# The statistics of three of four images move beside the first chunk's projections, and the last chunk prepares no successor

## The reference

```python
xn = layernorm(gn(x)) * ln_w + ln_b              # over channels
xb, z = split(xn @ w_in.T)                       # 384 -> 2 x 768
xc = silu(causal_conv4(xb) + conv_b)
dt, B, C = split(xc @ w_x.T)                     # 24, 16, 16
dt = softplus(dt @ w_dt.T + dt_b)
h = exp(dt * A) * h + (dt * xc) * B              # 16 states for each of 768 channels, along 4096 steps
y = (sum_n h * C + xc * D) * silu(z)
x = x + y @ w_out.T
x = x + attention(gn(x))                         # 8 heads of 48, windows of 64 positions, and a projection
```

## Time and profile before

| | us |
|---|---|
| median of 3 runs (6865.48 to 6866.52) | 6866.09 |
| the profiled execution, its own time | 6863.25 |
| its span | 6861.5 |
| two statistics blocks at the start | 0 to 74 |
| preparation of chunk 0 | 74 to 187.7 |
| 32 chunks of scan, 167.3 on average | 187.7 to 5542 |
| output of chunk 31, statistics | 5542 to 5574 |
| attention | 5574 to 6861.5 |

### The profile page before, as it was taken

One profiled execution on the slowest core, in us unless ns is written; L12 is line 12 of the kernel. 1 busy time (PEld: TensorE's weight loads), 2 busy tenths in 40 slices (PEclk: granted clock), 3 DMA queues, 4 the chain that ended last, 5 costly groups with the idle time before them and its releaser, 6 DMA issues. The chain is left out here.

```text
span 6861.5 us, 99209 instructions
## 1 busy us (share of the span) xinstructions
PE 5990.6 (87%) x32906; PEld 3756.6 (55%) x32906; DVE 6138.1 (89%) x7731; ACT 4716.2 (69%) x8759; POOL 5351.3 (78%) x4333
## 2 busy tenths in 40 slices
PE   4888888888888888888888888888888879999998
PEld 2455555555555555555555555555555547777776
DVE  4899999999999999999999999999999956666665
ACT  1777777777777777777777777777777743333332
POOL 0999999999999999999999999999999930101010
PEclk9999999999999999999999999999999989999999
DMA  4322222222222222222222222222222232222222
GB/s 186 114 112 111 112 109 112 102 101 101 100 102 101 101 101 103 104 101 102 100 101 102 100 101 104 104 101 102 101 101 101 108 125 71 78 79 77 81 73 68
DMA packets 177702, 694.99 MB, mean 101 GB/s; under 512 B 28332, under 2 KB 28556, under 8 KB 143140
## 3 DMA queue, kind: packets, MB, share of 16 engines
q1 hardware_dynamic: 177188, 688.65, 27.0%
HBM read 512.57 MB, written 157.09 MB: 98 GB/s over the span
## 5 line engine op out<-in xcount | busy, mean ns | idle before, releaser
L774 POOL TENSOR_TENSOR dbx<-u,bb 128x512 f32<-128x512 f32 x3072 | 3829.4, 1280 | 29.9 <-DVE p_da L673 14.8
L673 DVE TENSOR_TENSOR_SCAN p_da<-p_da,state_v,dbx 128x512 f32<-128x512 f32 x2112 | 2620.8, 1273 | 54.6 <-ACT p_da L548 54.6
L548 ACT ACTIVATE p_da<-dt,neg_a 128x512 f32<-128x512 f32 x3076 | 2076.1, 687 | 83.6 <-DVE h L680 8.2
L898 PEld LDWEIGHTS p_yt<-ident,hc_v 128*128 128x128 f32 x8448 | 1108.8, 151 | 1137.1 <-issue 843.0
L898 PE MATMUL p_yt<-ident,hc_v 128*128 128x128 f32 x8448 | 1381.5, 293 | 162.9 <-DVE hc_v L689 162.4
L689 DVE TENSOR_TENSOR hc_v<-cc,p_da 128x512 f32<-128x512 f32 x2112 | 1391.4, 666 | 0.0
L783 POOL TENSOR_TENSOR hc_g<-h,cc 128x512 f32<-128x512 f32 x960 | 1227.6, 1279 | 108.4 <-DVE h L680 108.3
L680 DVE TENSOR_TENSOR_SCAN h<-p_da,state_g,dbx 128x512 f32<-128x512 f32 x960 | 1218.1, 1269 | 103.8 <-ACT p_da L548 103.5
L839 PE MATMUL p_g<-xs,win 128*128 128x512 f32 x2376 | 1208.6, 603 | 74.7 <-ACT zt L500 36.3
L554 ACT ACTIVATE state_v<-p_da 128x1 f32<-128x1 f32 x2112 | 351.0, 166 | 914.2 <-DVE hc_v L689 901.8
L1321 POOL TENSOR_TENSOR x_low<-axn,x_upper 128x512 fp32r<-128x512 f32 x96 | 127.3, 1355 | 1045.9 <-DVE x_upper L1273 1045.9
(11 more groups left out here) (153 smaller groups left out, 7397.5 us busy)
## 6 DMA issues: line engine op xcount, KB each, us to landing
bb<-bc_spill SPq DMA_DIRECT2D x132, 1024.0 KB, 10.4
cc<-bc_spill SPq DMA_DIRECT2D x132, 1024.0 KB, 10.2
xc_spill<-xc SPq DMA_DIRECT2D x99, 512.0 KB, 2.6
z_spill<-zt SPq DMA_DIRECT2D x99, 512.0 KB, 3.9
xj<-xc_spill SPq DMA_DIRECT2D x193, 256.0 KB, 4.1
zj<-z_spill SPq DMA_DIRECT2D x192, 256.0 KB, 2.7
xs<-in_x SPq DMA_DIRECT2D x34, 768.0 KB, 5.7
xc<-in_x SPq DMA_DIRECT2D x33, 768.0 KB, 11.9
```

Of the source, the lines that this page charges most:

```text
L548: nc.scalar.activation(p_da[n % RD][:], dt[:, d % 2, :], ACT.Exp, scale=neg_a[:, d, n:n + 1])\
L673: nc.vector.tensor_tensor_scan(psum, psum, dbx[:, n % RB, :], state_v[:, d, k:k + 1], ALU.mult, ALU.add).then_inc(s_scan, 1)
L774: nc.gpsimd.tensor_tensor(dbx[:, n % RB, :], u[:, d % 2, :], bb[:, n, :], ALU.mult)\
L898: last = nc.tensor.matmul(p_yt[d % 2][:, b * P:(b + 1) * P], product[:, b * P:(b + 1) * P], ident[:], start=False, stop=n == NS - 1, is_tr ...
```

## The change

`input_statistics` becomes `constants` and loads nothing; the block of `group_affine` "in" is gone. In `scan_layer` SP first loads `win`, `lnb`, `lnw`, then the 8 tiles of image 0 into eight slots that lie in `bb` (5) and `cc` (3), `x[0]`, the other eight weights, and then the 24 tiles of the other images, of which tile c waits until VectorE is done with tile c - 8. VectorE takes image 0's statistics and its affine (part 0) ahead of `scale(0)`, and the 72 statistics instructions of the other images after `normalise(0)`, while TensorE and ScalarE do chunk 0's projections. Their affine (part 1) is put into chunk 0's scan, at g = 0, 2, 5 on VectorE, 1 on TensorE, 4 on ScalarE. SP fills `bb` and `cc` for chunk 0 when all statistics are done. The load of x[1] moves from ahead of `xj` to behind the first quarter of B, and `scale(1)` behind the first four decays. The pass i = 31 leaves out all that it did for a 33rd chunk, and `load_residual(NCH)` waits for x1 of chunk 31 alone.

```diff
--- before.py
+++ after.py
+AFFINE_STEPS, AFFINE_AT = 1 + 1 + 3 + 1 + 2, (0, 1, 2, 4, 5)
...
         gsc = ctx.enter_context(nc.sbuf_tensor("gsc", [P, NCH], F32))
         gbi = ctx.enter_context(nc.sbuf_tensor("gbi", [P, NCH], F32))
-        input_statistics(nc, x, ident, quarter, mean_w, eps_col, stats)
-        group_affine(nc, "in", stats, quarter, eps_col, gsc, gbi)
+        constants(nc, ident, quarter, mean_w, eps_col, stats)
-                   xc_d, z_d, bc_d, x1_d, ident, mean_w, eps_col, stats, gsc, gbi)
+                   xc_d, z_d, bc_d, x1_d, ident, quarter, mean_w, eps_col, stats, gsc, gbi)
...
-def input_statistics(nc, x, ident, quarter, mean_w, eps_col, stats):
-    RX = 4
+def constants(nc, ident, quarter, mean_w, eps_col, stats):
...
+        x_slots = [bb[:, NJ * r:NJ * r + NJ, :] for r in range(5)] + [cc[:, NJ * r:NJ * r + NJ, :] for r in range(3)]
+        RX = len(x_slots)
...
+        af_m, af_v = p_g[1][:, 0:NBATCH], p_g[1][:, NBATCH:2 * NBATCH]
...
-        N_LOADS = 11
+        N_LOADS = 8
...
         def _(sp):
+            def load_stat_x(c):
+                if c >= RX:
+                    sp.wait_ge(s_sd, (c - RX + 1) * NJ)
+                sp.dma_start(x_slots[c % RX], x[c]).then_inc(s_sx[c % RX], 16)
+            for dst, src in ((win, w_in), (lnb, ln_b), (lnw, ln_w)):
+                sp.dma_start(dst[:], src).then_inc(s_wi, 16)
+            for c in range(CPB):
+                load_stat_x(c)
             sp.dma_start(xs[:], x[0]).then_inc(s_xl, 16)
-            for dst, src in ((win, w_in), (wx, w_x), (wdt, w_dt), (wout, w_out), (cw, conv_w), (cb, conv_b),
-                             (dtb, dt_b), (dsk, d_skip), (neg_a, a_log), (lnw, ln_w), (lnb, ln_b)):
+            for dst, src in ((wx, w_x), (wdt, w_dt), (wout, w_out), (cw, conv_w), (cb, conv_b),
+                             (dtb, dt_b), (dsk, d_skip), (neg_a, a_log)):
                 sp.dma_start(dst[:], src).then_inc(s_w, 16)
+            for c in range(CPB, NCH):
+                load_stat_x(c)
...
-                sp.wait_ge(s_xm, i + 1)
-                for k in range(2):
-                    sp.wait_ge(s_xcs[k], i * 16 + 16)
+                if i < NCH:
+                    sp.wait_ge(s_xm, i + 1)
+                    for k in range(2):
+                        sp.wait_ge(s_xcs[k], i * 16 + 16)
+                else:
+                    sp.wait_ge(s_os, i * 16)
                 sp.dma_start(back, x[(i + (NCH - 1)) % NCH]).then_inc(s_rl, 16)
...
             for k in range(3):
                 store_silu(0, k)
-            load_x(1, 1)
             sp.wait_ge(s_xcs[0], 16)
             sp.dma_start(xj[:], xc_d[0, :, 0, :]).then_inc(s_xjl, 16)
             store_bc(0)
             sp.wait_ge(s_bcs, 16)
+            sp.wait_ge(s_sd, NCH * NJ)
             for k in range(4):
                 load_b(0, k)
+                if k == 0:
+                    load_x(1, 1)
...
-                    if 2 <= d < 5:
+                    if 2 <= d < 5 and q < NCH:
                         store_silu(q, d - 2)
-                    if d == 5:
+                    if d == 5 and q == NCH:
+                        load_zj(i, d)
+                    elif d == 5:
                         load_xj(q, 0)
-                        load_x(q + 1, (q + 1) % NCH)
+                        if q + 1 < NCH:
+                            load_x(q + 1, q + 1)
                         store_bc(q)
                         sp.wait_ge(s_bcs, q * 16 + 16)
...
+            def affine(part):
+                act.wait_ge(s_afm, 2 * part + 2)
+                images = slice(0, 1) if part == 0 else slice(1, NBATCH)
+                nc.scalar.activation(af_rs[:, images], af_v[:, images], ACT.Ln, bias=eps_col[:, 0:1]).then_inc(s_afa, 1)
+                act.wait_ge(s_afa, 2 * part + 1)
+                nc.scalar.activation(af_rs[:, images], af_rs[:, images], ACT.Exp, scale=-0.5).then_inc(s_afa, 1)
+            affine(0)
+            act.wait_ge(s_afd, AFFINE_STEPS)
             for j in range(NJ):
                 scale(0, j)
             act.wait_ge(s_w, 16 * N_LOADS)
@@ -571,12 +600,12 @@
                 if k % 6 == 5:
                     silu(0, k // 6)
             copy_xd(0)
-            for j in range(NJ):
-                scale(1, j)
             softplus(0, 0)
             skip(0, 0)
             for n in range(RD):
                 decay(0, 0, n)
+            for j in range(NJ):
+                scale(1, j)
...
-                        else:
+                        elif after[0] < NCH:
                             decay(*after, n + RD - NS)
+                        if i == 0 and d * NS + n == AFFINE_AT[3]:
+                            affine(1)
                         if n == COPY_Y_AT:
                             copy_y(i, d)
-                        if n == SOFTPLUS_AT:
+                        if n == SOFTPLUS_AT and after[0] < NCH:
                             softplus(*after)
-                        if n == SKIP_AT:
+                        if n == SKIP_AT and after[0] < NCH:
                             skip(*after)
                         g = d * NS + n
-                        if g in SCALE_AT:
+                        if g in SCALE_AT and q + 1 < NCH:
                             scale(q + 1, SCALE_AT.index(g))
+                        if q == NCH:
+                            continue
...
+            def input_stats(c):
+                dve.wait_ge(s_sx[c % RX], c // RX * 16 + 16)
+                for j in range(NJ):
+                    at = (c + 1) * (NJ * 6) + j * 6
+                    nc.vector.bn_stats(stats[:, at:at + 6], x_slots[c % RX][:, j, :]).then_inc(s_sd, 1)
+            def affine_means(part):
+                first, last = (0, 1) if part == 0 else (1, NBATCH)
+                dve.wait_ge(s_sd, last * CPB * NJ)
+                for b in range(first, last):
+                    at, per = (b * CPB + 1) * (NJ * 6), CPB * NJ * 6
+                    nc.vector.bn_aggr(af_mv[:, b, :], stats[:, at:at + per]).then_inc(s_afd, 1)
+                done = part * AFFINE_STEPS + last - first
+                dve.wait_ge(s_afd, done)
+                nc.vector.tensor_copy(af_mean[:, first:last], af_mv[:, first:last, 0]).then_inc(s_afd, 1)
+            def affine_variance(part):
+                at = slice(0, 1) if part == 0 else slice(1, NBATCH)
+                done = part * AFFINE_STEPS + (2 if part == 0 else NBATCH)
+                dve.wait_ge(s_afm, 2 * part + 1)
+                nc.vector.tensor_tensor(af_dev[:, at], af_mv[:, at, 0], af_m[:, at], ALU.subtract).then_inc(s_afd, 1)
+                dve.wait_ge(s_afd, done + 1)
+                nc.vector.tensor_tensor(af_sq[:, at], af_dev[:, at], af_dev[:, at], ALU.mult).then_inc(s_afd, 1)
+                dve.wait_ge(s_afd, done + 2)
+                nc.vector.tensor_tensor(af_sq[:, at], af_sq[:, at], af_mv[:, at, 1], ALU.add).then_inc(s_afd, 1)
+            def affine_result(part):
+                first, last = (0, 1) if part == 0 else (1, NBATCH)
+                at = slice(first, last)
+                done = part * AFFINE_STEPS + (5 if part == 0 else NBATCH + 3)
+                dve.wait_ge(s_afa, 2 * part + 2)
+                nc.vector.scalar_tensor_tensor(out=af_bi[:, at], in0=af_m[:, at], scalar=-1.0, in1=af_rs[:, at],
+                                               op0=ALU.mult, op1=ALU.mult).then_inc(s_afd, 1)
+                dve.wait_ge(s_afd, done + 1)
+                for dst, src in ((gsc, af_rs), (gbi, af_bi)):
+                    wide = src[:, at].rearrange("p (b o) -> p b o", o=1).to_broadcast([P, last - first, CPB])
+                    nc.vector.tensor_copy(dst[:, first * CPB:last * CPB].rearrange("p (b c) -> p b c", c=CPB), wide)\
+                        .then_inc(s_afd, 1)
+            for c in range(CPB):
+                input_stats(c)
+            affine_means(0)
+            affine_variance(0)
+            affine_result(0)
+            dve.wait_ge(s_wi, 16 * 3)
+            dve.wait_ge(s_prepm, 1)
+            for j in range(NJ):
+                nc.vector.tensor_scalar(win[:, j, :], win[:, j, :], lnw[:, j:j + 1], None, ALU.mult)\
+                    .then_inc(s_prep, 1)
             for j in range(NJ):
                 centre(0, j)
             dve.wait_ge(s_w, 16 * N_LOADS)
@@ -706,13 +789,12 @@
                 for k in range(TAPS):
                     nc.vector.tensor_scalar(cdiag[:, t, k, :], ident[:], cw[:, t, k:k + 1], None, ALU.mult)\
                         .then_inc(s_prep, 1)
-            dve.wait_ge(s_prepm, 1)
-            for j in range(NJ):
-                nc.vector.tensor_scalar(win[:, j, :], win[:, j, :], lnw[:, j:j + 1], None, ALU.mult)\
-                    .then_inc(s_prep, 1)
             dve.wait_ge(s_prep, N_PREP)
             for j in range(NJ):
                 normalise(0, j)
+            for c in range(CPB, NCH):
+                input_stats(c)
...
                             keep_state(i, d, BY_POOL.index(n) // RH)
```

(46 more changed lines are left out.)

36 lines of the change are left out of this document (16 added, 20 removed).

## The result

The changed kernel takes 6805.52 us (median of 5, 6802.13 to 6807.46), the one before 6866.09 in the same session: 60.6 us less, a ratio of 0.991 (95% interval 0.9896 to 0.9924). Forecast: 6805, with 60.9 us of gain.

What follows compares the result with a forecast made beforehand. VectorE was taken to bound the scan loop, and a serial one-engine-at-a-time chain the first 187.7 us. 61.2 + 3.0 - 7.0 + 3.0 + 0.7 = 60.9 us off the median 6866.1 gives 6805.2; 8-in-10 range 6797 to 6814.

Steps and rivals of the forecast that it cites:

- Statistics of image 0: Opening: eighth tile loaded at 26.9 us, its statistics done at 28.8, affine with one bn_aggr done at 32.6.
- cover of the bias matmuls: Opening: 72 bias matmuls end near 27, before TensorE's first affine matmul at 29.7; 2.7 us to spare.
- To the first in_step: From the affine's end to the first in_step: 51.9 us against 113.1, gain 61.2; clock -3 to +3.
- The other 24 tiles: 45 us of VectorE statistics after the first in_step, ending at 97, due near 117: hidden, cost nothing.
- So 0, up to 2: SP's first store queued behind statistics loads, issued 7 us late, landing 4 to 7 us after issue: cost 0 to 2 us.
- B, C and x[1]: Ahead of the first scan: B's first quarter no longer behind x[1]'s 768 KB; gain 3.0 us, bounds 0 and 4.
- The later quarters come 1 us sooner, which the next item hides: B and C loads for chunk 0: later quarters come 1 us sooner, not 3, hidden by the affine's part 1.
- Affine, part 1: Chunk 0's pass: 3.3 us added VectorE work plus 3.7 us wait for mean at centre; loss 7.0, bounds 3.3 and 9.
- The last pass: No 33rd chunk prepared: VectorE's work falls below GpSimd's; gain 3.0 us, between 0 and 6.2.
- The clock rival: Last pass and tail: TensorE's clock drops, VectorE waits 1 us a gate, tail loses 2.0; 6811 us, chance 0.15.
- The tail: After the loop: load_residual(NCH) no longer queued behind broadcasts, so residual starts earlier; gain 0.7 us.
- Passes 1 to 30: Scan loop between chunk 0's pass and the last: no change, 0 us.

Runs made afterwards that it cites:

- run 5: Changed kernel with win, lnb and lnw loaded behind image 0's eight tiles and x[0]; 6819.5 us, first scan 13.3 us later.
- run 8: Changed kernel with VectorE's six operations of 0.6 us put back into the last pass, results unused; last pass 163.0 us against 159.9, time 6804.40.
- run 4: Changed kernel with the first store of xc and zt put ahead of the last three statistics loads on SP; 6807.95 us, first scan 2.1 us earlier.
- run 2: Changed kernel with mean(1) ahead of the affine part 1's second matmul on TensorE; pass 0 172.9 us instead of 176.1, time 6802.66.
- run 9: Changed kernel once more, without any edit; 6806.22 us.
- run 1: Kernel before the change with only the 33rd chunk left out, opening not edited; 6863.45 us against 6865.21, ratio 0.9996.
- run 3: Changed kernel with the affine's part 1 taken out of chunk 0's scan and put ahead of it; 6797.32 us (median of 4), pass 0 170.7 us.
- run 6: Changed kernel with affine part 1 ahead of the scan, plus x[1]'s load moved behind the second store of xc and zt; 6795.68 us, pass 0 166.6.
- run 10: Changed kernel with every statistics instruction of the 24 tiles of images 1 to 3 done twice; 6830.93 us, first scan 27.7 us later.

## Why the prediction was right, step by step

- **Statistics of image 0.** Right: aggregate at 28.89 (28.8), affine done at 32.7 (32.6), cover of the bias matmuls 2.2 (2.7), its price shown by run 5.
- **To the first in_step.** 1.6 us better than forecast, all of it TensorE's clock: `mean` took 4.71 us instead of 5.49, `variance` 4.5 instead of 5.5. The text had set 3 us aside for this. In the other executions with this opening the first in_step came at 50.3 to 51.1.
- **The other 24 tiles.** Right that they hide: VectorE was done at 92.9. "So 0, up to 2" for SP's queue: taken at 0, it was 1.7 where TensorE kept the clock that it had before (run 8 against run 4), within the bound. The landing was mis-sized, 9.6 us where 4 to 7 stood; the copy was 3.7 us late in run 8, and TensorE's second bank took about half of that.
- **B, C and x[1].** In the first profile 1.9 of the "gain 3.0" came: from the copy of `xd` on, 61.0 us of lead became 62.9. That profile was an unlucky one. From the copy of `xd` to the first scan it took 11.0 us, and runs 2, 5, 8 and 9, with the same code there, 10.1 to 10.3; the kernel before took 12.9 and run 1, alike there, 13.1. So the gain is 2.6 to 3.0, as forecast. The +0.1 of the table is the 1.9 less the 1.8 that the projections lost (run 4). The store of B and C took 3.4 to 3.5 us, not 3.0, and was issued 0.5 us later in the first profile than in those four. Why it took longer than 3.0 is not shown; the last stores of `xc` and `zt` were issued just ahead of it. "The later quarters come 1 us sooner, which the next item hides" was right that they were hidden, and missed that x[1] among them was itself a delay of 4.1 us for whoever takes the cover away (runs 3 and 6).
- **Affine, part 1.** Right in mechanism, short by 2.5 us: 9.5 where 7.0 stood, beyond the bound of 9. The centre's wait was as reckoned, 3.9 for 3.7 (run 2 takes back 3.3). Missing were the wait for ScalarE's result, 1.4 us, and 0.7 us of work, 4.0 where 3.3 stood, as the sum at L758 took 1.1 us. Work and both waits add up to 9.3 of the 9.5. Why that sum is slow in the loop no run shows; ahead of the loop it took 0.16 us on the same three columns (run 3).
- **The last pass.** Right in sign, 5.0 for 3.0, within the bounds. VectorE's own work counts nearly in full (run 8). The reason given for stopping at 3.0, that VectorE's work falls below GpSimd's, did not come about: 160.8 us against 159.4 in the window of 162.3. The clock rival was right about the clock, 0.70, and wrong about its price: VectorE waited 0.3 us for TensorE in the whole pass.
- **The tail.** The DMA's wait is gone, but in the first profile the twelve passes took 8.43 us, for the most part at the lower clock. Net nothing there, and 1.4 us more were lost behind it. Both depend on the execution. Of the eleven traces with this tail, seven have the twelve passes at 8.4 to 8.5 us, and four, runs 2, 3, 8 and 10, at 6.8 to 6.9. In those four `residual` starts 13.3 to 13.4 us behind the last scan (15.0 in the seven, 14.9 before), and from there to the end it takes 1309.7 to 1310.1 us (1311.5 to 1311.7 in the seven, 1310.1 before). Between 60 and 100 us behind the last scan the granted clock is 0.95 in the four and 0.87 in the seven. So the gain of 0.7 was real and more, up to 1.6, when the clock was up, and this stretch alone moves the time by over 3 us. What decides between the two is not shown. `residual` in run 2:

```profile
5491.19 0.69 DVE L691 TENSOR_TENSOR xc<-xc,p_g 128x512 f32<-128x512 f32 x1 [6.92 <-PE p_g L963]
```

- **Passes 1 to 30.** Unchanged but for 0.8 us: after a disturbed pass the next ones are shorter (166.6, 166.9, 167.2, then 167.25). Executions of kernels alike in these passes differ by up to 5.4, so the 0.8 says nothing of the change.

## What to carry to other kernels

Work moved "beside" a serial stretch is cheap only if it stays out of the bound engine's stream behind it: here ten instructions of 0.14 to 1.1 us at the head of the loop made its first pass 9.5 us longer, and nothing was lost when they were put into the 31.8 us that VectorE idled just ahead of it and x[1] was out of the way too (run 6). Price a multi-engine chain by the waits it puts in front of what stands behind each of its links, on the transfer queue too: twice the statistics made not their own end late but a store that stood behind their loads. Once a wait is removed, look for the next one it had covered. And before a difference of 1 to 2 us in one trace is explained, look for other executions of the same code in that stage: two costs that overlap, like the store and the clock of run 4, do not add up.

## What the runs showed of the hardware

- The same program loses 1.7 us at a gate of pass 11 in one execution and not in another (run 9). In run 4 TensorE's granted clock was 0.58 at that place, just behind a wait of TensorE of 2.8 us; behind the same wait one pass earlier it was 1.00. Pass 24 is hit in every trace. A single hit was paid back within four or five passes; those of passes 11 and 14 in runs 2, 3 and 4 were not. Sums over passes 1 to 30 lay between 5015.6 and 5021.0 us in kernels alike in these passes, which is as much as the spread of the times.
- Twelve fp32 matmul passes of 512 columns behind the loop took 6.8 to 6.9 us in four executions and 8.4 to 8.5 us in seven; from 7 to 15 us behind the last scan the granted clock was 0.84 to 0.86 in the four and 0.64 to 0.65 in the seven.
- TensorE at 0.70 of its clock through a whole pass, and busy for 107 of 162 us, delayed VectorE by no more than 0.3 us.
- A 512 KB store landed 9.6 us after its issue when 768 KB loads stood ahead of it on the same queue, and 3.6 us after when none did.
